# Two heads' weights made by full-height matmuls on a zero-padded operand, one head a step, in place of two 64-row matmuls side by side

## What is computed

```python
s = jnp.clip(hs @ Ws1.T @ Ws2.T + bs2, -CLAMP, CLAMP)    # B, T, H, 64 slots
z = jax.lax.cumlogsumexp(s, axis=2)
es, enz = jnp.exp(s), jnp.exp(-z)
A  = jnp.einsum('bhtd,bhjd->bhtj', q, k) * scale         # causal
ok = (A masked) @ es * enz ; qv = softmax(ok over slots)
W  = causal mask of (qv * enz) @ es^T                    # T x T weights of one head
o  = W @ v ; o = rmsnorm(o) * w * silu(gate) ; y = o @ Wo.T
```

## Time and profile before

| | |
|---|---|
| median of 3 executions | 1764.04 us |
| lowest, highest | 1762.23 us, 1771.17 us |
| the profiled execution: its time | 1762.23 us |
| its span, first to last instruction | 1760.4 us |
| PE busy | 1624.6 us (92%) |
| DVE busy | 1283.4 us (73%) |
| ACT busy | 840.4 us (48%) |
| POOL busy | 554.6 us (32%) |
| chain that ended last | PE 75%, DVE 14%, issue 4%, ACT 4% |

### The profile page before, as it was taken

The page is one execution under the profiler, slowest core; times in us unless marked ns, Lnnn a source line. Parts: engine busy times, 40 slices in busy tenths (PEclk is TensorE's granted clock), DMA queues, the critical chain, the costliest instruction groups (busy, mean ns, idle before and its releaser), DMA issues.

```text
span 1760.4 us, 51382 instructions
## 1 busy us (share of the span) xinstructions
PE 1624.6 (92%) x21686; PEld 1145.0 (65%) x21686; DVE 1283.4 (73%) x2850; ACT 840.4 (48%) x1372; POOL 554.6 (32%) x949
## 2 busy tenths in 40 slices
PE   6999999999958899998999888998998899999989
PEld 5899999999743455554566555665454466666657
DVE  8877787788586888878898352443467798988954
ACT  3433433433441566556567712442243376776752
POOL 5454544534251222403302031541112123431230
PEclk9999999999988999999999979999999999999999
DMA  4010100110026553352462383562913036764200
GB/s 132 1 49 1 49 13 15 65 33 1 21 74 115 101 140 59 100 102 38 102 122 50 72 325 121 190 206 106 163 37 66 20 65 133 133 106 77 42 2 25
DMA packets 91856, 143.93 MB, mean 82 GB/s; under 512 B 14870, under 2 KB 60123, under 8 KB 91628
## 3 DMA queue, kind: packets, MB, share of 16 engines
q1 hardware_dynamic: 87228, 127.79, 31.6%
q10 hardware_dynamic: 2528, 7.74, 1.3%
q0 software_dynamic: 1872, 5.13, 0.8%
HBM read 109.68 MB, written 32.03 MB: 81 GB/s over the span
## 4 chain that ended last, share of the span: by engine, by line
PE 75%; DVE 14%; issue 4%; ACT 4%; POOL 1%; DMA 1%; another core or an unknown queue 1%; ACTq 0%; SPq 0%; POOLq 0%; DVEq 0%
PE bank L1002 22%; PE bank L1210 8%; PE bank L1959 5%; PE bank L1845 4%; PE bank L1847 4%; PE bank L1846 4%; PE bank L740 3%; PE bank L1978 3%; DVE xa_part_max L1283 3%; PE bank L2406 2%; PE bank L677 2%; DVE shared L1283 2%; PE bank L2421 1%; ACT xa_e L1244 1%; PE bank L704 1%
## 5 line engine op out<-in xcount | busy, mean ns | idle before, releaser
L1283 DVE TENSOR_REDUCE xa_part_max<-bank 128x1 f32<-128x448 f32 (+1 forms) x512 | 266.3, 568 | 22.3 <-PE bank L1002 19.5
L1244 ACT ACTIVATE xa_e<-bank 128x1024 f32<-128x1024 f32 (+1 forms) x208 | 211.7, 1023 | 107.5 <-PE bank L1002 105.9
L1244 ACT ACTIVATE ca_e<-bank 128x1024 f32<-128x1024 f32 (+2 forms) x208 | 197.8, 958 | 75.5 <-PE bank L1002 74.5
L1283 DVE TENSOR_REDUCE shared<-bank 128x1 f32<-128x400 f32 (+1 forms) x384 | 205.5, 570 | 21.3 <-PE bank L1002 18.0
L1002 PE MATMUL bank<-xa_kst,xa_qst 122*32 122x448 bf16 (+1 forms) x2048 | 177.5, 345 | 16.1 <-DVE xa_part_max L1283 7.7
L1210 PE MATMUL bank<-xa_e,xa_vaug 128*17 128x256 f32 (+1 forms) x1664 | 132.2, 383 | 4.7 <-ACT xa_e L1244 2.5
L1002 PE MATMUL bank<-xa_qst,xa_kst 128*32 128x256 bf16 (+1 forms) x3264 | 134.1, 274 | 0.0
L1210 PE MATMUL bank<-ca_e,ca_vaug 128*17 128x256 f32 (+2 forms) x1664 | 124.1, 365 | 7.0 <-issue 4.5
L938 POOL TENSOR_TENSOR gsa_qk<-gsa_qk,gsa_rot 128x512 f32<-128x512 f32 x64 | 81.8, 1278 | 138.1 <-DVE gsa_rot L856 138.1
L1002 PE MATMUL bank<-xa_wkv,shared 128*32 128x256 f32 (+1 forms) x1632 | 111.1, 393 | 5.6 <-DVE xa_r L1659 2.5
L1002 PEld LDWEIGHTS bank<-xa_qst,xa_kst 128*32 128x32 bf16 (+1 forms) x3264 | 92.9, 97 | 30.5 <-issue 3.0
(11 more groups left out here) (406 smaller groups left out, 4149.2 us busy)
## 6 DMA issues: line engine op xcount, KB each, us to landing
xa_kst<-xa_k_parts SPq DMA_DIRECT2D x96, 200.1 KB, 5.6
ca_kst<-ca_k_parts SPq DMA_DIRECT2D x96, 200.1 KB, 5.2
xa_k_parts<-xa_parts SPq DMA_DIRECT2D x24, 400.2 KB, 4.8
ca_k_parts<-moe_ctx_parts SPq DMA_DIRECT2D x8, 1200.8 KB
moe_gu<-in_expert_gate_up SPq DMA_DIRECT2D x8, 1024.0 KB
shared<-in_ctxT_split ACTq DMA_DIRECT2D x4, 1601.0 KB, 9.2
moe_ctxT<-in_ctxT SPq DMA_DIRECT2D x8, 800.5 KB, 8.0
ca_cv<-in_ctx SPq DMA_DIRECT2D x4, 1536.0 KB
```

The source lines that it names most:

```text
L1244: e.activation(self.e[m % 3][0:rows, :, first:T], banks[m % 2][0:rows].rearrange("p a (h t) -> p (a h) t", t=T)[:, :, first:T], ACT.Exp, s ...
L1283: e.tensor_reduce(top, work[:, 0:hi - lo], AX.X, ALU.max).then_inc(*reduced(t, *step))
```

## The change

- `qz` becomes two buffers of 128 x 2 x 256, one plane for each head. POOL sets them to zero once, at the start. The `z` step on ACT copies head 0's 64 partitions to plane 0 and head 1's to plane 1: two copies of 64 x 256 in place of one of 128 x 256. The other half of each plane stays zero.
- Each `w2` matmul now contracts over all 128 partitions, with both heads' `esT` as the stationary operand and the zero-padded plane of one head as the moving one. The stationary operand is loaded for each head.
- A `w2` step is now one head, `("w2", n, s)`, and takes one bank. The order is written anew: in the regular turn `("w2", p, 0), ("w2", p, 1)` stand where `("w2", p)` stood, and the pair p + 1 is taken apart, one head before `("o", p)` and one behind it. In the hand-written turns the head 0 halves are moved ahead, by between one and a dozen steps.

```diff
-        qz_all = sb("qz", [P, 4, T])
-        qz = [qz_all[:, i] for i in range(2)]
+        qz = [sb(f"qz{i}", [P, 2, T]) for i in range(2)]
...
-                    ("a", 7), ("cs", 1), ("v", 1, 0), ("qk", 9), ("v", 1, 1), ("z", 0), ("gate", 1), ("ok", 6), ("z", 1), ("norm_turn", 0, 7), ("ok", 7),
-                    ("sm_max", 1), ("w2", 0), ("qk", 10), ("a", 8), ("sm_exp", 1), ("a", 9), ("qk", 11), ("u", 3), ("o", 0), ("es", 3), ("cs", 2),
...
-                    ("gate", 3), ("scale", 0, 1), ("a", 11), ("z", 2), ("ok", 9), ("w_split", 1, "q"), ("ok", 10), ("w2", 2), ("z", 3),
...
+                    ("a", 7), ("cs", 1), ("v", 1, 0), ("qk", 9), ("v", 1, 1), ("z", 0), ("gate", 1), ("ok", 6), ("w2", 0, 0), ("z", 1), ("norm_turn", 0, 7), ("ok", 7),
+                    ("sm_max", 1), ("w2", 0, 1), ("qk", 10), ("a", 8), ("sm_exp", 1), ("a", 9), ("qk", 11), ("u", 3), ("o", 0), ("w2", 1, 0), ("es", 3), ("cs", 2),
...
+                    ("gate", 3), ("scale", 0, 1), ("a", 11), ("z", 2), ("ok", 9), ("w2", 2, 0), ("w_split", 1, "q"), ("ok", 10), ("w2", 2, 1), ("z", 3),
...
-                    ("scale", m - 3, 1), ("ot", m - 3, 0), ("qk", s + 2), ("gate", p + 1), ("w2", p),
-                    ("ok", s - 1), ("ot", m - 3, 1), ("cs", m), ("a", s), ("o", p),
-                    ("w2", p + 1), ("qk", s + 3), ("wo", m - 3, 0), ("et", m), ("sm_max", m - 1), ("a", s + 1),
+                    ("scale", m - 3, 1), ("ot", m - 3, 0), ("qk", s + 2), ("gate", p + 1), ("w2", p, 0), ("w2", p, 1),
+                    ("ok", s - 1), ("ot", m - 3, 1), ("cs", m), ("a", s), ("w2", p + 1, 0), ("o", p),
+                    ("w2", p + 1, 1), ("qk", s + 3), ("wo", m - 3, 0), ("et", m), ("sm_max", m - 1), ("a", s + 1),
...
-                    ("gate", 28), ("et", 15), ("ok", 62), ("scale", 13, 0), ("xk", 0, 0), ("scale", 13, 1), ("rr", 13), ("xk", 0, 1), ("xk", 0, 2),
-                    ("z", 29), ("w2", 28), ("norm_turn", 1, 0), ("a", 63), ("xk", 0, 3), ("xk", 0, 4), ("xk", 0, 5), ("xk", 0, 6), ("ot", 13, 0), ("xk", 0, 7),
+                    ("gate", 28), ("et", 15), ("ok", 62), ("scale", 13, 0), ("xk", 0, 0), ("scale", 13, 1), ("rr", 13), ("w2", 28, 0), ("xk", 0, 1), ("xk", 0, 2),
+                    ("z", 29), ("w2", 28, 1), ("norm_turn", 1, 0), ("a", 63), ("xk", 0, 3), ("xk", 0, 4), ("xk", 0, 5), ("xk", 0, 6), ("ot", 13, 0), ("xk", 0, 7),
...
-                    ("k_scale", 0, 6), ("z", 30), ("k_turn", 0, 1), ("k_scale", 0, 7), ("norm_stats", 1, 2, 4), ("norm", 1, 2), ("k_turn", 0, 2),
+                    ("k_scale", 0, 6), ("z", 30), ("w2", 30, 0), ("k_turn", 0, 1), ("k_scale", 0, 7), ("norm_stats", 1, 2, 4), ("norm", 1, 2), ("k_turn", 0, 2),
...
-            "z": [(on_act, z_ready)], "w2": [(on_act, w2_copied[0]), (on_act, w2_copied[1])], "ot": [(on_act, ot_ready)],
+            "z": [(on_act, z_ready)], "w2": [(on_act, w2_copied)], "ot": [(on_act, ot_ready)],
...
                 elif kind == "w2":
+                    s, = rest
                     unit, hp = divmod(n, 2)
                     tb, zb = esT[unit % 3], qz[n % 2]
                     q.wait_ge(z_ready, "z", n)
                     q.wait_ge(et_ready, "et", unit)
-                    heads = [(home(kind, j), slice(s * SLOTS, (s + 1) * SLOTS)) for s, (j, _) in enumerate(places)]
-                    for to, r in heads:
-                        e.matmul(to[:, 0:T], tb[r, hp, 0:P], zb[r, :], start=True, stop=True)
-                    for s, (to, r) in enumerate(heads):
-                        e.matmul(to[:, T:T + P], tb[r, hp, P:T], zb[r, P:T], start=True, stop=True).then_inc(*w2_mm(n, s))
+                    e.matmul(ps[:, 0:T], tb[:, hp, 0:P], zb[:, s, :], start=True, stop=True)
+                    e.matmul(ps[:, T:T + P], tb[:, hp, P:T], zb[:, s, P:T], start=True, stop=True).then_inc(*w2_mm(n, s))
...
                 elif kind == "z":
-                    if n >= 2:
+                    ps, zb = home(kind, j), qz[n % 2]
+                    if n < 2:
+                        q.wait_ge(qz_zeroed, n)
+                    else:
                         q.wait_ge(w2_mm, n - 2, 1)
                     q.wait_ge(z_mm, n)
-                    e.copy(qz[n % 2], home(kind, j)[:, 0:T]).then_inc(*z_ready(*step))
+                    e.copy(zb[0:SLOTS, 0, :], ps[0:SLOTS, 0:T])
+                    e.copy(zb[SLOTS:P, 1, :], ps[SLOTS:P, 0:T]).then_inc(*z_ready(*step))
                 elif kind == "w2":
+                    s, = rest
                     if n:
                         q.wait_ge(o_mm, n - 1)
-                    for s, (at_, _) in enumerate(places):
-                        q.wait_ge(w2_mm, n, s)
-                        e.copy(w2T[s][:], home(kind, at_)[:, 0:3 * P]).then_inc(*w2_copied[s](*step))
+                    q.wait_ge(w2_mm, n, s)
+                    e.copy(w2T[s][:], home(kind, j)[:, 0:3 * P]).then_inc(*w2_copied(*step))
...
+            for i, z in enumerate(qz):
+                e.memset(z[:], 0.0).then_inc(*qz_zeroed(i))
```

More of the change, by code:

```diff
@@ L453, in build @@
         X_KEYS[1] = lambda n: ("wo", (GROUPS - 1) * B + n // TB, n % TB)
-        zeroed = local("gsa", "zeroed")
+        zeroed, qz_zeroed = local("gsa", "zeroed"), local("gsa", "qz_zeroed")
         w_hi, w_lo, h_hi, h_lo, wo_scaled = (local("gsa", n) for n in ("w_hi", "w_lo", "h_hi", "h_lo", "wo_scaled"))
@@ L461, in build @@
         less_max, sm_exp, sm_sum, sm_ready = (local("gsa", n) for n in ("less_max", "exp", "sum", "sm"))
-        z_mm, z_ready, w2_mm, w2_ready = (local("gsa", n) for n in ("z_mm", "z", "w2_mm", "w2"))
-        w2_copied = [local("gsa", f"w2_copied{s}") for s in range(2)]
+        z_mm, z_ready, w2_mm, w2_copied, w2_ready = (local("gsa", n) for n in ("z_mm", "z", "w2_mm", "w2_copied", "w2"))
         g_mm, g_tanh, g_ready, o_mm = (local("gsa", n) for n in ("g_mm", "tanh", "gate", "o_mm"))
@@ L545, in last_turns @@
                     ("qk", 60), ("sm_exp", 13), ("ok", 56), ("v", 14, 0), ("a", 58), ("scale", 12, 0), ("es", 15), ("rr", 12), ("ok", 57), ("a", 59), ("xa_w", 2),
[5 rows of a table removed]
[7 rows of a table added]
                     ("q", 1), ("rr", 14), ("q_norm", 0), ("k_scale", 0, 0), ("k_scale", 0, 1), ("q_store", 0), ("k_scale", 0, 2), ("gate", 30), ("scale", 14, 0),
                     ("scale", 14, 1), ("k_scale", 0, 3), ("k_scale", 0, 4), ("k_turn", 0, 0), ("k_scale", 0, 5), ("wo", 13, 1), ("k_store", 0, 1, None), ("ot", 14, 0),
-                    ("k_scale", 0, 6), ("z", 30), ("k_turn", 0, 1), ("k_scale", 0, 7), ("norm_stats", 1, 2, 4), ("norm", 1, 2), ("k_turn", 0, 2),
-                    ("z", 31), ("k_scale", 0, 8), ("v", 15, 1), ("w2", 30), ("k_turn", 0, 3), ("xv", 0, 0), ("norm_turn", 1, 2), ("q_turn", 0), ("k_turn", 0, 4),
-                    ("k_turn", 0, 5), ("ot", 14, 1), ("k_turn", 0, 6), ("o", 30), ("k_scale", 0, 9), ("k_turn", 0, 7), ("gate", 31), ("k_scale", 0, 10),
-                    ("k_turn", 0, 8), ("norm", 1, 3), ("w2", 31), ("k_scale", 0, 11), ("wo", 14, 0), ("k_turn", 0, 9), ("k_store", 0, 2, None), ("q_turn", 1),
+                    ("k_scale", 0, 6), ("z", 30), ("w2", 30, 0), ("k_turn", 0, 1), ("k_scale", 0, 7), ("norm_stats", 1, 2, 4), ("norm", 1, 2), ("k_turn", 0, 2),
+                    ("z", 31), ("k_scale", 0, 8), ("v", 15, 1), ("w2", 30, 1), ("k_turn", 0, 3), ("xv", 0, 0), ("norm_turn", 1, 2), ("q_turn", 0), ("k_turn", 0, 4),
+                    ("k_turn", 0, 5), ("ot", 14, 1), ("k_turn", 0, 6), ("o", 30), ("w2", 31, 0), ("k_scale", 0, 9), ("k_turn", 0, 7), ("gate", 31), ("k_scale", 0, 10),
+                    ("k_turn", 0, 8), ("norm", 1, 3), ("w2", 31, 1), ("k_scale", 0, 11), ("wo", 14, 0), ("k_turn", 0, 9), ("k_store", 0, 2, None), ("q_turn", 1),
                     ("k_scale", 0, 12), ("wo", 14, 1), ("norm_turn", 1, 3), ("k_turn", 0, 10), ("k_turn", 0, 11), ("k_store", 0, 0, None), ("k_turn", 0, 12),
@@ L627, in gsa_pe @@
                 if places:
[L628 to L631, removed]
+                    (j, free), = places
+                    ps = home(kind, j)
+                    if free:
+                        q.wait_ge(*free)
                 if kind == "u":
@@ L945, in gsa_pool @@
                 elif kind == "w2":
-                    for s in range(2):
-                        q.wait_ge(w2_copied[s], *step)
-                        seen(w2T[s]).then_inc(*w2_ready(n, s))
+                    s, = rest
+                    q.wait_ge(w2_copied, *step)
+                    seen(w2T[s]).then_inc(*w2_ready(n, s))
                 elif kind == "scale":
```

## The result

The kernel after takes 1781.9 us (median of 10, 1773.29 to 1788.02) against 1763.5 us for the kernel before on the same chip (10, 1758.13 to 1771.17): a ratio of 1.0101, interval [1.0076, 1.0126]. The forecast was 1770 us and +0.41%. The profiled execution of after took 1770.01 us (span 1768.0), less than any of the ten timed ones. Against the profiled execution of before (1762.23 us) that is +7.8 us, close to the sum of the prediction; the timed ones are another 10 us away.

A forecast was written before the change was run, and what follows sets the result against it. PE's instruction stream was taken to bound GSA's regular turns. Terms 7.5 + 0.3 + 0.9 - 1.5 = +7.2 us gave 1769.4 on the profiled 1762.23 us, 1771.2 on the median; predicted 1770 us, range 1765 to 1776.

The forecast's parts named there:

- a turn: Sign in GSA's regular turns: 29.2 us in place of 28.7; wrong if growth is under 0.4 or over 0.7 us.
- the last turn: Sign at GSA's end: same stretch length up to the boundary; wrong if it moves by more than 3 us.
- PE's busy time up to 440 us: Sign in the new trace: PE's total busy time up to 440 us should grow by 7 to 8 us.
- The price of a step: Each `w2` step in GSA costs PE 0.26 us more; 29 steps ahead of 474 us make +7.5 us.
- The fourth rival: In `w2` steps the halves never ran side by side, so the change costs PE nothing: 1763 us; chance 0.04.
- The first rival's mechanism: `o`'s square behind the `w2` (p+1, 0) copy delays DVE's chain, up to 0.48 us a turn: 1776 us; slower side 0.33.
- Step 2: Early in GSA, PE waits for ACT's two `z` copies, idling 1.35 us: +0.9 us beyond the 0.26.
- step 30: Late in GSA, PE waits 1.5 to 2 us for ACT, ahead of 3.5 us of idle: 0, up to +1.7.
- `a` 63: In GSA's last turn, its 1.52 us wait for ACT's copy of `z` 29 goes: -1.5 us.
- the copies: On ACT, a second copy for each `z` adds 0.27 us, 8.6 us over 32, hidden while PE isn't waiting.
- GSA as a whole: All terms lie in this stage and sum to +7.2 us.
- "slower": Whole kernel slower by over 0.5%, from GSA's delayed DVE chain or a step's upper price; together chance 0.33.

The follow-up runs named there:

- order alone: Kernel before with the new order and one bank a head, but 64-row matmuls and one `z` copy: 1.0173 of the kernel before.
- height alone: Kernel before with full-height matmuls and two copies for each `z`, in the old order with two banks a step: 1.0052 of the kernel before.
- the experiment that moves it back: Kernel after with 28 extra PE instructions at the start and `w2` (2, 0) put back behind `ok` 10: 1769.01 us, a single execution.
- 228: Kernel before with 228 extra wait instructions at PE's start: 1.0133 of the kernel before.
- 256: Kernel before with 256 extra wait instructions at PE's start: 1.0110 of the kernel before.
- the new place: PE's code behind GSA stands 28 instructions earlier than in the kernel before (-28), as in the unpadded kernel after: 1.0070 to 1.0101.
- place 0: PE's later code stands where the kernel before has it; with 28 extra instructions at PE's start, after took 1.0061 and order alone 1.0121.
- the later two: The kernel after, unchanged, timed a second and a third time: 1.0070 and 1.0082 of the kernel before.
- Place -14: Kernel after with 14 extra instructions at PE's start, its later code half way between that of after and of before: 1.0105 of the kernel before.
- +28: Extra instructions at PE's start: kernel before with 28 took 1.0036, after with 56 1.0099, height alone with 28 1.0095, order alone with 56 1.0148.

## Why the prediction was wrong

By its own signs the prediction came true: a turn grew by 0.52 us (wrong under 0.4 or over 0.7), and from 446 us to the boundary DVE's offset against before only went from +8.3 to +7.9 us (the last turn was to move by no more than 3). None of its signs looks behind GSA. One of them could not have shown anything: PE's busy time up to 440 us was to grow by 7 to 8 us, but PE was busy throughout already, all 340 us from 100 to 440 in both kernels, so it could not.

**The price of a step** was right in size: 0.26 predicted, 0.26 measured (1.59 us against 1.33; a turn +0.52). Its reasoning was half wrong. The prediction said that the old halves overlap, but not fully, and that 0.1 us goes on either side for a change of height. The order alone shows full overlap and 64-row instructions that are slower by themselves (0.54 against 0.44 us for 256 columns), with about 0.1 us at either side. The fourth rival (never side by side) falls. A pack here costs 1.04 us whether it holds one head or two, and not the 0.65 us of a full-height head, so packing two heads is worth 0.26 us a pair and not 0.65. The Trainium skill (TensorE: Matmul & The Clock Gate, Part 3) says that each further tile of a pack adds only about 4 ns. The trace agrees (1.38 us with one head, 1.39 with two), and the prediction was wrong to take the 1.04 us as a sign against that.

**The first rival's mechanism** (DVE's chain behind the moved `o_sqr`) didn't happen: the turn grew by 0.52 us and not by 1.0, and height alone, with the old order, has the same turn.

**Step 2, step 30, `a` 63, the copies.** PE waits 1.30 us at step 2, worth 0.7 by the experiment that moves it back (0.9 forecast); from height alone to after, DVE is 0.7 us later behind it, too. The wait at step 30, put at 0, is followed by 0.4 us in DVE's offset, which is nearly gone by the boundary (+8.05 there, +7.9 at the end). `a` 63 gave back 1.1 us of the 1.5 (DVE's offset against before falls from +8.3 to +7.2 there). ACT's 32 further copies cost 0.366 us each, 11.7 in all and not 8.6: hidden, as said.

**GSA as a whole:** +7.9 us in the first pair of profiles against +7.2 forecast; 547.4 to 549.5 against 538.3 to 539.5 over all profiles of after and before (without 228 and 256), or +9.6 in the mean. I found no single place for the rest, and it stays open; one profile of after lost 1.6 us once in the first turns, and the kernel before scatters by 0.7 there.

**The step that failed** is the sum: it has no term for the stages behind GSA. It took their time as given since no line of them changes. At the new place the two cross attentions grew by 864.4 - 856.5 = 7.9 us in the mean, about as much as the price in the changed stage, and all stages behind GSA by 1224.3 - 1218.2 = 6.1. With +9.6 for GSA that makes 15.7 us, and 13.1 with the mean of after's own three profiles (1221.7); measured were 12.3, 14.4 and 17.8 (1.0070, 1.0082, 1.0101). Put back to place 0, after costs 1.0061, or 10.7 us (7.6 to 14.1), which the GSA term alone explains. The GSA term itself was 2.4 us too small. The chance of 0.33 for "slower" rested on other mechanisms, and neither was the cause. It couldn't have been read from the trace of before that the order would save 28 waits. That PE stops behind GSA without a cause that the profile names, twice at a distance of 128 matmuls (4042 and 4170), could have, and with the 172 packets of queue 8 it hints that these stops depend on the length of the code ahead of them.

**What stays open.** Why a stop is short at one place in the work and 2 to 4 us long at another: a block that ends while a large transfer runs (shared<-in_ctxT_split, 1601 KB, lands in 10.3 us in the second profile of after and in 7.9 in before) is a reason that I argued and didn't test. Nor is it known whether the late landing of xa_qst (5.1 against 3.0 us from issue) is a cause or a companion of the stop ahead of it. The first group's 1.0101 is above the later two; the intervals just overlap. Place -14 is short in its one profile, which is the fastest of its six executions, while its median is not. And for the kernel after itself the gain from the old place (1.0061 against 1.0070 to 1.0101) is inside the intervals: it rests on the profiles, and on height alone, order alone and the kernel before, where the timed executions do show the place.

No version here beats the kernel before; among the four places tried, its own is the best.

## What to carry to other kernels

An edit that changes the number of instructions on the bounding engine moves all the code behind it, and here that was worth about as much (6 to 9 us in 1760, where the timed executions are clear) as the edit's own effect. So before a few tenths of a per cent are put down to an edit, time it at the old place as well (pad at the start, under an idle stretch), and time a pad alone. One profiled execution can agree with a sum to 0.6 us and lie below every timed one: compare stages over several profiles, all of them and not only those that move as expected. And where two orders differ by side-by-side work, measure a lone half: it tells overlap from the price of the shape.

## What the hardware showed unexpectedly

- PE's code arrives in packets of 16,384 bytes, one for each 256 instructions (stops 128 matmuls apart, each with its weight load). A block end cost nothing that can be seen at most places, and up to 3.9 us at a few.
- A shift of 28 instructions to +28 costs 0.3 to 0.4%: clear for the kernel before (1.0000 to 1.0036) and for height alone (1.0052 to 1.0095), with intervals that touch for after (1.0061 to 1.0099) and overlap for order alone (1.0121 to 1.0148). To -28, order alone loses 0.5% (1.0121 to 1.0173), clear as well.
- Waits at PE's start that wait for nothing more aren't free: 228 instructions of two waits each moved its first matmul from 8.55 to 28.37 us, and 256 to 31.47: (31.47 - 28.37) / 28 = 0.11 us each.
- An f32 matmul over 64 rows, 256 columns, takes 0.54 us start to start, alone or with a second half beside it, against 0.44 over 128 rows.
- ACT's copy of 64 x 256 takes 365 to 368 ns and that of 128 x 256 takes 375: the number of partitions hardly counts.
